# A Flamingo block on one core: another order of the beginning, a first stack without DRAM, padded kv weights, later norms

## What is computed

```python
def _L0_xattn_ref(query, key, value, wq, bq, wk, bk, wv, bv):
    q = (query @ wq.T + bq).reshape(B, L, H, Dh).transpose(0, 2, 1, 3)
    ...                                   # k, v from ctx; 16 heads of 16
    attn = softmax(einsum('bhld,bhsd->bhls', q, k) / scale)
    return einsum('bhls,bhsd->bhld', attn, v)...

def _L0_ffn_ref(src, Wq, Wk_c, Wv_c, Wk, Wv, Wo, ...):
    q = src @ Wq ; k = src @ Wk_c @ Wk ; v = src @ Wv_c @ Wv
    ...                                   # rope on q and k, self-attention, @ Wo
    x = _rmsnorm(src + sa, norm1_w)
    ...                                   # shared net, and top-2 of 8 experts in 2 groups
    return _rmsnorm(x + shared + routed, norm2_w)

x = x + tanh(g_xattn[0]) * _L0_xattn_ref(_layernorm(x), ctx_1024, ctx_1024, ...)
x = x + tanh(g_ffn[0]) * _L0_ffn_ref(_layernorm(x), ...)
```

## Time and profile before

| | |
|---|---|
| median of 3 runs | 769.13 us (769.03 to 769.82) |
| the profiled execution, its own time | 769.24 us |
| its span, first to last instruction | 767.5 us |
| mean granted TensorE clock | 0.993 of full |
| PE busy | 734.2 us, 96% |
| DVE busy | 502.3 us, 65% |
| ACT busy | 412.9 us, 54% |
| first score pair | 31.74 us from the start |
| first score unit | 47.43 us |
| first pair of instance 1 | 80.26 us |

### The profile page before, as it was taken

The page is one execution under the profiler, slowest core; times in us unless marked ns, Lnnn a source line. Parts: engine busy times, 40 slices in busy tenths (PEclk is TensorE's granted clock), DMA queues, the critical chain, the costliest instruction groups (busy, mean ns, idle before and its releaser), DMA issues.

```text
span 767.5 us, 10227 instructions
## 1 busy us (share of the span) xinstructions
PE 734.2 (96%) x3468; PEld 333.6 (43%) x3468; DVE 502.3 (65%) x732; ACT 412.9 (54%) x792; POOL 217.8 (28%) x327
## 2 busy tenths in 40 slices
PE   7799999999999999999999999999999999999995
PEld 4442343243233233233423432424544756468884
DVE  3599848847878878878797789771566222532554
ACT  3357867858758767875775866676211122222111
POOL 5243132233325405303321510010104722400444
PEclk9999999999999999999999999999999999999998
DMA  8618443235214414512331233005102555000111
GB/s 265 181 43 269 103 132 106 81 91 172 64 50 163 112 42 124 151 43 84 125 83 41 97 111 85 1 1 184 36 1 98 208 174 179 7 0 1 35 35 42
DMA packets 49587, 73.31 MB, mean 96 GB/s; under 512 B 7552, under 2 KB 39552, under 8 KB 49536
## 3 DMA queue, kind: packets, MB, share of 16 engines
q1 hardware_dynamic: 45200, 63.80, 28.2%
q0 software_dynamic: 2816, 8.46, 2.9%
q10 hardware_dynamic: 1520, 0.40, 0.3%
HBM read 45.04 MB, written 27.33 MB: 94 GB/s over the span
## 4 chain that ended last, share of the span: by engine, by line
PE 69%; DVE 13%; ACT 5%; DMA 5%; issue 3%; POOL 2%; SPq 2%; POOLq 0%; DVEq 0%; ACTq 0%
PE ps L1507 30%; PE ps L1658 12%; PE ps L1694 11%; PE ps L1630 10%; DVE negm L1164 6%; ACT hS L923 3%; PE ps L1502 2%; POOL scrf L763 2%; DVE bst L1042 1%; DMA scrq<-mix 1%; PE ps L1564 1%; DMA w<-scrq 1%; PE ps L1644 1%; DMA wT<-in_L_xattn_wk_dram 1%; SPq L530 1%
## 5 line engine op out<-in xcount | busy, mean ns | idle before, releaser
L1164 DVE TENSOR_REDUCE negm<-ps 128x2 f32<-128x1024 f32 x256 | 303.5, 1220 | 71.6 <-PE ps L1630 64.8
L923 ACT ACTIVATE hS<-ps 128x512 f32<-128x512 f32 x512 | 280.1, 604 | 111.7 <-PE ps L1694 109.8
L1694 PE MATMUL ps<-w 98*128 98x512 bf16 x512 | 168.8, 383 | 6.0 <-ACT hS L923 2.6
L1630 PE MATMUL ps<-w 96*128 96x512 bf16 x512 | 153.4, 381 | 9.6 <-DMA w<-scrq 4.6
L1658 PE MATMUL ps<-hS,mix 128*17 128x512 f32 x1024 | 134.7, 598 | 0.2
L1694 PEld LDWEIGHTS ps<-w 98*128 98x128 bf16 x512 | 43.6, 96 | 157.1 <-ACT hS L923 94.8
L1630 PEld LDWEIGHTS ps<-w 96*128 96x128 bf16 x512 | 47.5, 98 | 61.3 <-issue 11.5
L1362 DVE SCALAR_TENSOR_TENSOR ctxs<-qk,ps 128x512 f32<-128x512 f32 x32 | 22.0, 687 | 72.9 <-ACT qk L959 72.1
L959 ACT ACTIVATE qk<-ps 128x512 f32<-128x512 f32 x32 | 19.1, 597 | 76.3 <-PE ps L1507 76.3
L1507 PE MATMUL ps<-w,hS 128*128 x256 | 55.6, 379 | 0.0
L1507 PEld LDWEIGHTS ps<-w,hS 128*128 128x128 f32 x256 | 48.6, 190 | 7.0 <-issue 0.5
(11 more groups left out here) (211 smaller groups left out, 858.1 us busy)
## 6 DMA issues: line engine op xcount, KB each, us to landing
w<-scrq SPq DMA_DIRECT2D x32, 384.0 KB, 4.3
scrk<-mix SPq DMA_DIRECT2D x24, 256.0 KB, 2.2
scrq<-mix SPq DMA_DIRECT2D x16, 384.0 KB, 3.3
w<-scrk SPq DMA_DIRECT2D x32, 192.0 KB, 2.9
scrq<-mix SPq DMA_DIRECT2D x24, 256.0 KB, 2.5
w<-scrk SPq DMA_DIRECT2D x32, 128.0 KB, 2.9
w<-in_L_ffn_W_experts_dram SPq DMA_DIRECT2D x8, 512.0 KB, 8.2
mix<-scrf SPq DMA_DIRECT2D x4, 528.0 KB, 4.1
```

The lines of the kernel that those rows point to most:

```text
L923: nc.scalar.activation(prob[:, kt % PROB_SLOTS, s % HG, :], slot_bank(("unit", u)), ACT.Exp, scale=SC).then_inc(s_exp, 1)
L1164: V.tensor_reduce(negm[:, gi % 2, h, 2 * t2:2 * t2 + 2], ps[:, bank:bank + 2, :], AX.X, ALU.max, negate=True).then_inc(s_re, 1)
L1630: last = MM(ps[:, bank + t, :], qs[0:STK, g, h, tt * P:(tt + 1) * P], ks[0:STK, g, h, :], start=True, stop=True)
L1694: MM(o, ks[:, g, h, kt * P:(kt + 1) * P], qs[:, g, h, :], start=True, stop=True).then_inc(s_sT, 1)
```

## The change

**1. Layout and first stack.** `dims_first` now orders features as (group, dim, head in group), so that half 0 has groups 0 and 1. Group 0's stack of instance 0 is filled from SBUF to SBUF by 12 DMAs (`direct`, 16 rows by 4 heads x 512, 64 KB each), each issued when its part of half 0 is there, ahead of the puts. In the four cross instances the scratch is now read as [term, dim, 4 heads x 512]: the rows stay 4 KB, but term and dim no longer lie at one stride. The self instances read as before.

**2. Norm and parts of instance 0.** For x0 the statistics are aggregated on DVE (`bn_aggr`), POOL adds and takes the power, DVE normalises in four instructions and copies turned tile 1 (ACT copies tile 0). Parts are made by half: part 0 on ACT; remainders on DVE in the order K0, Q0, K1, Q1; parts 1 and 2 of half 0 on DVE, part 1 of half 1 on ACT, part 2 of half 1 on POOL. Memsets of ones write pairs of bf16 as one f32.

**3. Fills.** 46 at the start, none later.

**4. Pieces of batch 1.** Keys' projection first, a piece ahead of each pair but the first, two ahead of pair 5; the first maxima are turned ahead of pair 10 (before: of pair 9). ACT issues max rows 0 before the last pieces, and the tanh of the gates comes behind.

**5. Loads.** wk goes to ACT's queue; the 15 weight loads go behind the reads of group 1.

**6. fkv** is now two tiles of 128 rows, the other half zero (two more memsets), and its products contract over 128 rows.

**7. Norm steps.** `fastats` and `nf` of batches 0 to 2 now stand in the last instance at steps 42 to 56.

```diff
-FILL, FILL_STACK, FILL_ROWS = 24, 12, 10
+FILL = 46
...
-        ("fatile", 3, 23), ("faempty", 3, 23), ("fastats", 0, 32), ("nf", 0, 43)]
+        ("fatile", 3, 23), ("faempty", 3, 23)]
+    NORM_STEPS = [("fastats", 0, 42), ("nf", 0, 46), ("fastats", 1, 47), ("nf", 1, 51), ("fastats", 2, 52), ("nf", 2, 56)]
...
+    for what, b_, step in NORM_STEPS:
+        hook(NI - 1, step, what, b_, 0)
+    BEGIN = [[0, 1, 6, 4, 7, 5, 8, 9], [6, 7, 0, 1, 4, 5, 8, 9]]
+    N_DIRECT = 2 * NTERM
...
-            for j in (1, 0, 2):
+            for j in (0, 2):
...
+            def load_weights():
+                for d_, s_ in small:
+                    sp.dma_start(d_, s_, allow_slow_non_contiguous=True).then_inc(s_ws, 16)
+                for d_, s_ in large:
+                    sp.dma_start(d_, s_).then_inc(s_w, 16)
...
+                def direct(X, part):
+                    sp.wait_ge(s_hp[part][X], 1)
+                    for r in range(NTERM):
+                        if (K_PART if X else Q_PART)[r] == part:
+                            sp.dma_start((ks if X else qs)[r * DH:(r + 1) * DH, 0], parts[X][0:P // 2, part, 0, :]).then_inc(s_dir, 16)
...
-                def heads(scr, terms, g):
-                    return scr[par, 0:terms].rearrange("r (d h) t -> (r d) h t", h=NH)[:, g * HG:(g + 1) * HG]
+                def stack_rows(at, scr, terms, g):
+                    if INST[n][0] == "c":
+                        heads = scr[par, 0:terms].rearrange("r (g d h) t -> g r d (h t)", g=NG, h=HG)[g]
+                        sp.dma_start(at.rearrange("p h l -> p (h l)"), heads).then_inc(s_stk[g], 16)
+                    else:
+                        heads = scr[par, 0:terms].rearrange("r (d h) t -> (r d) h t", h=NH)[:, g * HG:(g + 1) * HG]
+                        sp.dma_start(at, heads).then_inc(s_stk[g], 16)
...
-                    for part in range(NPART):
-                        put(1, part, ready[part])
-                    put(0, 0, ready[0])
+                    for X in (1, 0):
+                        for part in range(NPART):
+                            direct(X, part)
+                    for X in (1, 0):
+                        for part in range(NPART):
+                            put(X, part, ready[part])
                     sp.wait_ge(s_scr[1], SCR[1])
-                    keys(0)
-                    put(0, 1, ready[1])
-                    put(0, 2, ready[2])
+                    keys(1)
                     sp.wait_ge(s_scr[0], SCR[0])
-                    queries(0)
-                    sp.wait_ge(s_stk[0], 64)
-                    keys(1)
                     queries(1)
+                    load_weights()
...
+            def begin_third(X):
+                pool.wait_ge(s_p1[X], 1)
+                link(pool.tensor_tensor(parts[X][:, 2, 1, :], qk[X][:, 1, :], parts[X][:, 1, 1, :], ALU.subtract))
+                pool.wait_ge(s_hp[2][X], 1)
+                pool.sem_inc(s_spl[X], 1)
...
+                pool.wait_ge(s_var, 1)
+                link(pool.tensor_scalar(nvar[:], mv[:, :, 1], 1e-5, None, ALU.add))
+                pool.tensor_tensor(scale_[:, 0, :], nvar[:], mhalf[:], ALU.pow).then_inc(s_ny["x"], 1)
...
+            act.dma_start(wT[:, 1], wk).then_inc(s_wn[1], 16)
...
+            def begin_part(X, o):
+                nc.scalar.activation(parts[X][:, 0, o, :], full(("proj", 0, 4 + 2 * X + o)), ACT.Identity,
+                                     bias=bqk[:, X, o:o + 1]).then_inc(s_p0[X] if o else s_hp[0][X], 1)
+            def begin_second_part(X):
+                act.wait_ge(s_r0[X], 1)
+                nc.scalar.activation(parts[X][:, 1, 1, :], qk[X][:, 1, :], ACT.Copy).then_inc(s_p1[X], 1)
...
+            for i in range(2):
+                V.memset(fkv[i][(1 - i) * DC:(2 - i) * DC, :], 0.0).then_inc(s_ini, 1)
...
+            def begin_norm():
+                dve.wait_ge(s_ldx[0], 16)
+                statistics(0, "x", xin[0])
+                for tt in range(TT):
+                    mark(V.bn_aggr(mv[:, tt, :], bst[:, 0, tt, :]))
+                settle()
+                dve.sem_inc(s_var, 1)
+                dve.wait_ge(s_ny["x"], 1)
+                for tt in range(TT):
+                    V.tensor_scalar(src[0][:, tt, :], xin[0][:, tt, :], mv[:, tt, 0:1], scale_[:, 0, tt:tt + 1], ALU.subtract,
+                                    ALU.mult).then_inc(s_src, 1)
+                V.tensor_copy(nT[:, 1, :], full(("proj", 0, 1))).then_inc(s_tv, 1)
...
+            def begin_rest(X, o):
+                key = ("proj", 0, 4 + 2 * X + o)
+                dve.wait_ge(s_p0[X] if o else s_hp[0][X], 1)
+                V.scalar_tensor_tensor(out=qk[X][:, o, :], in0=full(key), scalar=bqk[:, X, o:o + 1],
+                                       in1=parts[X][:, 0, o, :], op0=ALU.add, op1=ALU.subtract).then_inc(s_tv, 1)
+                dve.wait_ge(s_tv, EMPTIED[key][1])
+                if o:
+                    dve.sem_inc(s_r0[X], 1)
+                    return
+                link(V.tensor_copy(parts[X][:, 1, 0, :], qk[X][:, 0, :]))
+                dve.sem_inc(s_hp[1][X], 1)
+                link(V.tensor_tensor(parts[X][:, 2, 0, :], qk[X][:, 0, :], parts[X][:, 1, 0, :], ALU.subtract))
+                dve.sem_inc(s_hp[2][X], 1)
...
-                if q == LEAD - 4:
+                if q == LEAD - 2:
                     cross_values(1, 0)
-                if q == LEAD - 2:
                     cross_values(1, 1)
...
-                    last = MM(o, fkv[0:DC, f * P:(f + 1) * P], cT[0:DC, 0, :], start=True, stop=True)
+                    last = MM(o, fkv[0][:, f * P:(f + 1) * P], cT[:, 0, :], start=True, stop=True)
                 else:
                     emptied(("proj", m, 4))
                     for j in range(2):
                         tt = 2 * (t - 7) + j
-                        last = MM(o[:, j * D:(j + 1) * D], cT[DC:2 * DC, 0, tt * P:(tt + 1) * P], fkv[DC:2 * DC, :],
-                                  start=True, stop=True)
+                        last = MM(o[:, j * D:(j + 1) * D], cT[:, 0, tt * P:(tt + 1) * P], fkv[1][:], start=True, stop=True)
...
-                    pe.wait_ge(s_stk[g], (gi // NG + 1) * 64)
+                if q == 0:
+                    pe.wait_ge(s_dir, 16 * N_DIRECT)
+                elif p == 0:
+                    pe.wait_ge(s_stk[g], (gi // NG + (g > 0)) * 64)
...
-            second = [(cross_tile, 1, t) for t in range(CT)] + [(second_query, o, c) for o in range(2) for c in range(CT)]
-            second += [(second_value, h, t) for h in range(2) for t in range(2)]
-            between = {2: 2, 3: 1, 4: 1, 5: 1, 6: 1, 8: 2, 9: 1, 10: 1}
-            fill(ps[:, 5, :], FILL_STACK)
...
             for q in range(LEAD - 1):
-                for f, a, b in second[:between.get(q, 0)]:
-                    f(a, b)
-                del second[:between.get(q, 0)]
-                if q == PAIRS // NG + 1:
+                if q == LEAD - 2:
                     turn_max(0)
-                if q == 0:
-                    emptied(("proj", 0, 9))
+                pieces(between.get(q, 1))
                 max_pair(q)
-            assert not second
+            pieces(len(second))
...
-                        if u == 0:
-                            fill(o, FILL_ROWS)
...
-    return w.reshape(-1, nh, w.shape[-1] // nh).transpose(0, 2, 1).reshape(w.shape)
+    return w.reshape(-1, nh // HG, HG, w.shape[-1] // nh).transpose(0, 1, 3, 2).reshape(w.shape)
```

More of the change, by code:

```diff
@@ L127, in flamingo_block @@
         SLOTS.extend(("proj", m_, t_) for t_ in BEGIN[m_])
-    SLOTS.append(("turned", 0))
+    SLOTS.insert(SLOTS.index(("proj", 1, 8)), ("turned", 0))
     for u_ in range(NI * UNITS):
@@ L239, in flamingo_block @@
         fkvc = sb("fkvc", [P, CT, 2 * DC], F32)
-        fkv = sb("fkv", [P, D], F32)
+        fkv = [sb(f"fkv{i}", [P, D], F32) for i in range(2)]
         fo = sb("fo", [P, CT, D], F32)
@@ L361, in flamingo_block @@
         s_bv = sem("value_bias_loaded")
-        s_hp = [sem(f"first_half_part{i}") for i in range(2)]
+        s_hp = [[sem(f"first_half_part{r}_{i}") for i in range(2)] for r in range(NPART)]
+        s_dir = sem("first_stack_loaded")
+        s_var = sem("first_variance_ready")
         s_id = sem("identity_steps")
@@ L485, in _ @@
                 (fq[:], f_wq),
-                (fkv[0:DC, :], f_wk),
+                (fkv[0][0:DC, :], f_wk),
             )
             assert len(small) == N_SMALL
-            for d_, s_ in small:
-                sp.dma_start(d_, s_, allow_slow_non_contiguous=True).then_inc(s_ws, 16)
             large = [
@@ L876, in self_tile @@
                         act.sem_inc(s_vp, 1)
[L878 to L882 removed]
+            def begin_part(X, o):
[4 more added lines that the diff above has]
+                nc.scalar.activation(parts[X][:, 1, 1, :], qk[X][:, 1, :], ACT.Copy).then_inc(s_p1[X], 1)
             def begin():
[L885 to L886 removed]
+                cross_tile(0, 0)
                 act.wait_ge(s_wb, 16 * N_BIAS)
```

(39 more changed lines are left out.)

94 lines of the change are left out of this document (40 added, 54 removed).

## The result

The changed kernel takes 788.11 us (median of 4, 786.50 to 791.25) against 769.08; the ratio is 1.025, 95% interval 1.0232 to 1.0269. It is slower, as forecast, but by 19 us instead of 2.4, and outside the range of 755 to 780. The profiled execution took 786.73, its span is 785.0; before they were 769.24 and 767.5, so the trace holds 17.5 us of the loss.

What follows compares the result with a forecast made beforehand. PE, busy 96% of the span, was taken as the bound, so edits pay where it idles, slows or has less work. 769.24 + 4.7 + 1.5 - 2.4 - 1.5 = 771.5 us, own range 764 to 777, with rivals 755 to 780.

Steps and rivals of the forecast that it cites:

- narrow reads: Cross-instance stack reads: only as many DMA engines as the outermost dimension allows share a read, lowest engine 196 KB, before 48.
- L: Data time of one cross-instance stack on its lowest engine: 7.5 us instead of 1.8; 2.0 for issue and latency came on top.
- the meeting point: First pair of instance 1 (pair 32), at 80.26 before; its shift prices the new beginning: +4.7 us, bounds +2.6 and +7.0.
- query reads of group 1 issued: Second group's stack in instance 0: last query part ready near 23.7, put landing 3.3 later, so reads issued at 27.0.
- first pair of instance 1: Pair 32, two stacks after stack 3's issue at 53.7: at 85.0, the middle of 82.9 and 87.3.
- narrow and slow: Rival, cross-instance stack reads: an engine gives only 20.5 GB/s, L = 9.8, pair 32 at 92.1, total 778.6; chance 0.16.
- a small rival: Beginning: the 12 direct DMAs are late, first pair at 25; costs only with wide reads, 758; chance within wide reads' 0.22.
- wide reads: Rival, cross-instance stack reads: spread over 16 engines as before, L stays 1.8, first unit at 37.0, total 754.9; chance 0.22.
- The weights were costed at nothing: Beginning: the 15 weight loads behind the reads of group 1 go out while SP has nothing else to issue; no cost.
- The clock: Beginning: PE's three or four waits of 2 to 7 us lower its clock behind them: +1.5 us, bounds nothing and 3.4.
- The later edits: fkv with 128 rows -2.4 us; norm steps 2.8 gained, less 1.3 lost waiting for last heads at the end, net -1.5.
- The rule that was weighed: DMA engines: the largest number up to 16 dividing both sides' slowest dimensions, the lowest-numbered ones, carry a transfer.

Runs made afterwards that it cites:

- e1_wide: The kernel after with stack rows ordered (dim, term), so that every cross-instance stack read has 16 as outermost dimension: 763.35 us, ratio to before 0.9898.
- e8_after_large_later: The kernel after, narrow reads kept, with the ten large weight loads behind the reads of group 2 instead of group 1: 790.55 us, ratio to before 1.0266.

## Why the prediction was wrong in size

The direction and its mechanism held: narrow reads. The steps that failed are sizes: the price of a narrow stack, 2.0 + L = 9.5 us from issue to landing, where stack 2 took 11.8 and stack 3 13.1, and four costs that the sum left out or put at nothing (SP's issues ahead of the puts, the weights beside stack 1, the clock behind the meeting point, the max rows behind narrow reads). Up to the meeting point:

| term | forecast | measured | rows |
|---|---|---|---|
| query reads of group 1 issued | 27.0 | 31.28 | SP |
| stack 1 landed | +7.5 | +10.6 | 31.28 to 41.86 |
| max rows 0 landed, group 2 issued | +6.1 | +6.2 | 48.04 |
| stack 2 landed | +9.5 | +11.9 | 59.90 |
| stack 3 issued | +3.6 | +3.1 | 63.03 |
| first pair of instance 1 | +31.3 | +31.6 | 94.59 |
| sum | 85.0 | 94.6 | |

- **The time of a stack was mis-sized.** I took L = 7.5 for the data, at 26.8 GB/s for an engine, and 2.0 around it. The rate was near right: with two engines at work it is 25, which gives 8.0 for the 200.7 kB. What failed is the 2.0, which was 3.8 in stack 2. The first packet of data starts 1.6 us behind the first issue (49.60), so that the lowest engine's mean rate from there to the landing is 19.6. The kernel before shows it already: its stack 2 took 5.3 (47.26 to 52.56), where 2.0 + 1.8 is 3.8. The rival "narrow and slow" comes to 2.0 + 9.8, just what stack 2 took, but by luck: it has all of the error in the rate. Its sum, 778.6, was still low.
- **SP's issues ahead of the puts were left out**, the largest single error, 4.3. The last part was ready at 23.54, as forecast (23.7):

```profile
22.38 1.16 POOL L703 TENSOR_TENSOR mix<-qk,mix 128x512 bf16<-128x512 f32 x1 [0.92 <-ACT mix L920]
```

But SP issues its 12 direct DMAs and 8 puts back to back from 14.10 to 28.03; the direct ones take 7.71 of it, so the puts begin at 21.85. The last put goes out at 27.31, 3.6 late, and lands 4.0 later instead of 3.3. I had named the direct DMAs, as a small rival, for the first pair alone: it was 23.65, where I said 21.5.
- **The same two errors stand in the rival "wide reads"**, which said 754.9, or 758 with late direct DMAs. With wide reads in fact, in e1_wide, stack 1 is ready at 37.18 instead of 30.0 and the first unit at 44.43 instead of 37.0, and the kernel takes 763.35.
- **The weights were costed at nothing** because SP had nothing else to issue. SP was not the resource: the 15 loads were in flight together with stack 1. e8_after_large_later puts the ten large ones at 1.6 us for stack 1, and shows why moving them did not help.
- **The clock** fell as said, but by more: between the pair at 94.59 and unit 48 another 3.0 us are lost (8.3 instead of 5.3), against 1.5 in the sum. Part of it is a wait for max rows.
- **A step that is not in the prediction at all:** the max rows wait behind the narrow reads, in the other cross instances too:

```profile
102.91 0.59 PE L1738 MATMUL ps<-w 98*128 98x512 bf16 x2 [1.07 <-DMA w<-mTs]
...
153.94 0.59 PE L1738 MATMUL ps<-w 98*128 98x512 bf16 x2 [2.10 <-DMA w<-mTs]
```

So 3.3 us are lost from unit 48 to 192; in e1_wide nothing of it is left (-3.4 to -3.5). The 8 KB that the second of these units waits for, issued at 147.65, landed at 153.80, 6.2 us later; the same rows of e1_wide took 2.0 (126.96 to 128.96).
- **The later edits were right.** 5.2 foreseen (2.4 and 2.8), 5.3 found; apart they gave 2.3 and 3.1. The end cost 2.1 where I said 1.3 (its own terms, 533.6 against 532.83 less 0.4, come to 1.2). The row of norms stands in DVE's timeline as foreseen, 7 us each from statistics to last multiplication (528.48 to 535.27), compare:

```profile
528.48 1.41 DVE L1082 BATCH_NORM_STATS2 bst<-rows 128x6 f32<-128x256 f32 x4
533.60 1.67 DVE L1089 SCALAR_TENSOR_TENSOR rows<-rows,scale,n_bc 128x256 f32<-128x256 f32 x4 [3.71 <-POOLq L684]
```

and on PE, after the last unit:

```profile
550.36 1.06 PE L1548 MATMUL ps<-identf,hS 128*128 128x128 f32 x8 [2.00 <-DVEq L1240]
```

The account of the profiled execution: 769.24 + 17.4 + 3.3 - 5.3 + 2.1 = 786.7. Counted from the forecast: 771.5 + 9.6 up to the meeting point + 1.5 of clock and max rows behind it + 3.3 of max rows + 0.8 at the end - 0.1 = 786.6. The median is 1.4 above the profiled execution: the kernel after spreads over 4.8 us from run to run, the kernel before over 0.8 beside it, and over 3.8 in all its runs for the experiments (768.21 to 771.99).

- **The rule that was weighed** held. The Trainium skill ("DMA: Bandwidth & Descriptors", "Why a DMA increments its semaphore by 16 and not by 1") says that only the engines in use signal their landing. The semaphore records of the trace hold 30 increments for a narrow stack (27 engines' shares, 3 + 2 + 16 + 6, and one more for each of the three narrow reads) and 64 for a stack of the self instances. It told the narrow reads from the wide rightly; between the forecast and "narrow and slow" it could not decide.

## What to carry to other kernels

Look at the outermost dimension of both sides of every DMA when a layout changes: with 3 or 2 or 6 there instead of 48, the bytes, rows and line lengths are the same and a 768 KB stack takes 12 us instead of 5. Putting the 16 outermost, by another order of rows that nobody else sees, turned a loss of 2.5% into a gain of 1%. A transfer moved to where its queue is idle still costs if someone waits for what its DMA engines also carry. Count the issues of a queue as well as its bytes. And a chain of reads that each wait for the last pays an error in one of them several times.
